# Sharing one value tile between two batches in the cross-attention of a Perceiver block

## The chip, the cores and the metric

One NeuronCore of a Trainium2 chip runs the whole block as one program. The metric is device time in microseconds, the median of several runs. The engines are TensorE (PE; its weight loads are shown apart as PEld), VectorE (DVE), ScalarE (ACT), GpSimd (POOL) and SyncE (SP, which only issues DMAs here).

## The reference, cut to what matters

```python
x = x + _L0_xattn_ref(_layernorm(x), ctx_1024, Wq, bq, Wkv, bkv, Wout, bout)   # x (16, 64, 512), ctx (16, 1601, 512)
x = x + _L0_attn_ref(_layernorm(x), ...)       # linear attention over 64 rows of each batch
x = x + _L0_ffn_ref(_layernorm(x), ...)        # 8 experts, top 2

def _L0_xattn_ref(query, context, ...):        # 16 heads of 32
    q = query @ Wq + bq
    kv = context @ Wkv + bkv                   # k and v interleaved in the last axis
    scores = jnp.einsum('bhid,bhjd->bhij', q, k) * SCALE
    attn = jax.nn.softmax(scores, axis=-1)
    out = jnp.einsum('bhij,bhjd->bhid', attn, v)
    return out @ Wout + bout
```

The change touches only the computation of `v = context @ Wv`: 16 batches of 1601 context rows each.

## The kernel before

The cross-attention takes most of the time, and it is the only part touched (`cross_attention`, L186 to L1111). All large products are made in float32r in three passes: both operands are split into a rounded part (hi) and a rest (lo), and hi*hi, hi*lo and lo*hi are added up in PSUM.

**Context.** A batch has 1601 rows, loaded transposed in four chunks of 384, 384, 384 and 450 columns into `ctx_raw`; VectorE rounds a chunk into `ctx_hi` (L577), GpSimd subtracts to get `ctx_lo` (L493).

**Units.** Keys and values of a batch are made in NU = 29 units of twelve matmuls (4 slices of the model dimension, three passes; L960). 16 are K units (a chunk times 128 dimensions, moving operand 384 or 450 columns). 13 are V units (L953 to L958): there the context tile is the stationary operand, 128 context rows, and the 512 columns of Wv move. 1601 = 12 x 128 + 65, so the 13th V unit has only 65 stationary columns (`TAIL`, `rows`). A unit writes one of two PSUM banks in turn (`ps_kv`); ScalarE copies it out to `k_t` or `v` (`copy_unit`, L818 and L822). A unit waits for the copy of the unit two before it (L944). The semaphores `kv_done` and `kv_copied` count units, 29 to a batch.

**Pairs.** The attention of a batch goes through 8 pairs of heads. For pair p of batch b TensorE does, in this order (`batch`, L1008 to L1027): transposes of the probabilities, groups 0, 1 and 2 (`turn`), the scores of the next pair (`scores`, L974), the transposes of group 3, and the product with the values (`values`, L986). In the four gaps it does units of the *next* batch: one K unit after group 0, one after group 1, a V unit after group 3, and in some pairs a second V unit after the product. Which pairs have two is in `BEHIND` (L92): the 1st, 3rd, 5th, 7th and 8th. The last chunk's units stand in the 7th and 8th pair: V units 9 and 10 in the 7th, 11 and 12 (the tail) in the 8th. ScalarE copies the V units of a pair right after the exponential of the next pair (L857 to L860).

**Beside it.** VectorE in a pair: the outputs of the pair before (L596 to L601, which free the PSUM bank `ps_o` for transpose group 1), the rests of the four probability groups (L652), the row maximum (L636), the rounding of the keys of two pairs on (`k_parts`, L588), and in the 1st, 3rd, 5th and 7th pair the rounding of a context chunk (L577). GpSimd: the rest of the values (`v_parts`, L516), the rest of the keys (L504), the rest of the context chunk (L493). SyncE issues the loads, each behind the wait that frees its buffer, strictly in the order of its queue.

**Start.** The units of batch 0 (`START`) run before any attention, with the layer norm, its transposes and the query projection between them (`start_steps`, L313). The queries go to DRAM (L471) and come back as blocks (`load_q`, L389); `FIRST_SCORES` = 26 is the unit ahead of which the first scores are made. Batch 0 then runs alone, batches 1 to 14 in a loop of 7 rounds of two, and batch 15 in `last_batch`.

## Time and profile before

| | |
|---|---|
| median of three runs | 2359.82 us (2358.14 to 2363.23) |
| the profiled execution | 2358.58 us, span 2356.8 us |
| granted TensorE clock, mean | 0.987 |
| TensorE busy | 2274.6 us, 97% |
| VectorE, ScalarE, GpSimd busy | 57%, 44%, 47% |
| start, batches, rest | to 124 us; 124 to about 1840 us; to the end |

In the rows below a time is in microseconds from the start of the span. A timeline row has the start, the duration, the engine, the line, the operation with output<-inputs and shapes, and how often it stands in a row; in brackets is the idle time of the engine before it and what ended it. A matmul's duration is modelled to its end, so in a stream of matmuls the distance of two starts tells what one costs.

### The profile page before, as it was taken

Reading aid. Unit: us, or ns where it says so; the run is one execution under the profiler, and the core shown is the slowest. Engines: PE = TensorE matmul, PEld = TensorE weight load, DVE = VectorE, ACT = ScalarE, POOL = GpSimd, SP = SyncE. Lnnn points to the kernel's source line nnn. Section 1 sums busy time; section 2 is a strip of 40 time slices with the busy share of each in tenths; the row PEclk is TensorE's granted clock in tenths of the full one; section 3 lists DMA queues with packets and bytes.
Section 4 is the critical chain, followed back from the end, with each engine's and each line's share of the span. In section 5 each row is a group of like instructions: output and inputs, shape, how many; then the busy total and the mean of one; then the engine's idle time right before and its main releaser. Section 6 shows DMA issues by size and latency. Waiting matters only on the chain. (4 is left out here: it accounts for less than half of the span.)

```text
span 2356.8 us, 37225 instructions
## 1 busy us (share of the span) xinstructions
PE 2274.6 (97%) x12921; PEld 1981.8 (84%) x12921; DVE 1348.1 (57%) x2112; ACT 1036.2 (44%) x1737; POOL 1105.3 (47%) x454
## 2 busy tenths in 40 slices
PE   8999999999999999999999999999998897799997
PEld 7688889888888889888888888888875686788886
DVE  3155655565655656565656556565667546756653
ACT  3154444444444444444444444444444421545443
POOL 2155455454455455555555555555556202533333
PEclk9999999999999999999999999999999998999999
DMA  4212111121111112111121111121131102855654
GB/s 145 96 48 57 51 48 46 49 63 50 48 47 48 45 53 66 48 46 49 47 58 52 51 48 45 53 62 52 46 114 37 39 20 103 248 172 187 193 157 92
DMA packets 141464, 175.61 MB, mean 75 GB/s; under 512 B 81600, under 2 KB 105024, under 8 KB 141248
## 3 DMA queue, kind: packets, MB, share of 16 engines
q1 hardware_dynamic: 132352, 147.37, 20.8%
q10 hardware_dynamic: 4608, 16.78, 2.2%
q0 software_dynamic: 4288, 8.67, 1.7%
q8 instruction: 125, 2.05, 0.4%
q14 instruction: 91, 0.75, 0.1%
HBM read 135.12 MB, written 37.65 MB: 73 GB/s over the span
## 5 line engine op out<-in xcount | busy, mean ns | idle before, releaser
L504 POOL TENSOR_TENSOR k_parts<-k_t,k_parts 64x1602 fp32r<-64x1602 f32 x128 | 436.9, 3413 | 717.3 <-DVE k_parts L588 717.3
L960 PE MATMUL ps_kv<-ctx_hi,wk_hi 128*128 128x384 f32 (+1 forms) x1024 | 376.0, 367 | 8.8 <-DVE ctx_lo L785 8.8
L652 DVE TENSOR_TENSOR probs_t<-ps_pt,probs_t 128x512 fp32r<-128x512 f32 x376 | 207.6, 552 | 275.4 <-ACT probs_t L830 273.9
L960 PE MATMUL ps_kv<-ctx_lo,wk_hi 128*128 128x384 f32 (+1 forms) x1024 | 352.9, 345 | 0.0
L960 PE MATMUL ps_kv<-ctx_hi,wk_lo 128*128 128x384 f32 (+1 forms) x1024 | 352.9, 345 | 0.0
L960 PE MATMUL ps_kv<-wv_hi,ctx_hi 128*128 128x512 f32 (+1 forms) x832 | 343.0, 412 | 0.6 <-DVE wv_lo L755 0.6
L960 PE MATMUL ps_kv<-wv_lo,ctx_hi 128*128 128x512 f32 (+1 forms) x832 | 330.6, 397 | 0.0
L960 PE MATMUL ps_kv<-wv_hi,ctx_lo 128*128 128x512 f32 (+1 forms) x832 | 326.4, 392 | 0.0
L838 ACT ACTIVATE probs_both<-ps_s,neg_max 128x1601 f32<-128x1601 f32 x128 | 205.0, 1602 | 178.8 <-DVE neg_max L638 178.8
L818 ACT ACTIVATE k_t<-ps_kv,bk_sb 128x384 f32<-128x384 f32 (+1 forms) x256 | 152.5, 596 | 293.3 <-PE ps_kv L960 293.2
L493 POOL TENSOR_TENSOR ctx_lo<-ctx_raw,ctx_hi 128x1536 fp32r<-128x1536 f32 (+1 forms) x64 | 233.4, 3647 | 86.0 <-DVE ctx_hi L577 84.6
L516 POOL TENSOR_TENSOR v_parts<-v,v_parts 128x832 fp32r<-128x832 f32 x120 | 237.3, 1977 | 70.4 <-ACT v_parts L848 57.2
L830 ACT CAST probs_t<-ps_pt 128x512 fp32r<-128x512 f32 x376 | 178.3, 474 | 190.5 <-PE ps_pt L1005 175.6
L636 DVE TENSOR_REDUCE row_max<-ps_s 128x1 f32<-128x1601 f32 x128 | 233.5, 1824 | 22.0 <-PE ps_s L974 9.2
L822 ACT COPY v<-ps_kv 128x512 f32<-128x512 f32 (+1 forms) x208 | 120.8, 581 | 278.3 <-PE ps_kv L960 278.3
L986 PEld LDWEIGHTS ps_o<-probs_t,v_parts 128*128 128x128 f32 (+1 forms) x1664 | 214.4, 190 | 19.8 <-DVE probs_t L652 8.9
L974 PE MATMUL ps_s<-k_parts,q_blocks 128*128 128x512 f32 (+2 forms) x1024 | 221.4, 359 | 5.1 <-DMA q_blocks<-q_parts 4.2
L986 PE MATMUL ps_o<-probs_t,v_parts 128*128 128x256 f32 (+1 forms) x1664 | 218.6, 282 | 7.5 <-DVE probs_t L652 7.5
L652 DVE TENSOR_TENSOR probs_t<-ps_o,probs_t 128x512 fp32r<-128x512 f32 x128 | 88.5, 691 | 229.7 <-ACT probs_t L830 229.5
L960 PEld LDWEIGHTS ps_kv<-ctx_hi,wk_hi 128*128 128x128 f32 x1024 | 193.6, 189 | 13.2 <-issue 9.5
L960 PEld LDWEIGHTS ps_kv<-ctx_lo,wk_hi 128*128 128x128 f32 x1024 | 194.4, 190 | 3.8 <-issue 0.7
L1005 PE MATMUL ps_pt<-ident,probs_both 128*128 128x128 f32 x1120 | 190.5, 278 | 6.0 <-DVE probs_t L652 3.8
(315 smaller groups left out, 4071.7 us busy)
## 6 DMA issues: line engine op xcount, KB each, us to landing
ctx_raw<-ctx_dram SPq DMA_DIRECT2D x49, 768.0 KB, 4.6
w_raw<-w_dram SPq DMA_DIRECT2D x64, 512.0 KB
rows_in<-zeros SPq DMA_DIRECT2D x150, 128.0 KB, 4.0
w_raw<-w_dram ACTq DMA_DIRECT2D x32, 512.0 KB
ctx_raw<-ctx_dram SPq DMA_DIRECT2D x16, 900.0 KB, 4.8
q_blocks<-q_parts SPq DMA_DIRECT2D x256, 32.0 KB, 2.3
rows<-rows_in SPq DMA_DIRECT2D x8, 768.0 KB
q_parts<-probs_t SPq DMA_DIRECT2D x16, 256.0 KB, 2.0
```

The lines of the kernel that those rows point to most:

```text
L493: nc.gpsimd.tensor_tensor(ctx_lo[c % 2][:, 0:w], ctx_raw[c % 2][:, 0:w], ctx_hi[c % 2][:, 0:w].bitcast(F32), ALU.subtract).then_inc(ctx_lo ...
L504: nc.gpsimd.tensor_tensor(k_parts[64 - 64 * s:128 - 64 * s, :], k_t[par][64 * s:64 * s + 64, g, :], k_parts[64 * s:64 * s + 64, :].bitcast ...
L516: nc.gpsimd.tensor_tensor(v_parts[:, :, 1, :], v[par][:, :, 64 * p:64 * p + 64], v_parts[:, :, 0, :].bitcast(F32), ALU.subtract).then_inc( ...
L636: nc.vector.tensor_reduce(row_max[:, q:q + 1], ps_s[:, S0:S0 + LC], AX.X, ALU.max).then_inc(max_done, 1)
L652: nc.vector.tensor_tensor(probs_t[0:m, j:j + k, 1, :], ps_turned[kv][g][0:m, 0:k, :], probs_t[0:m, j:j + k, 0, :].bitcast(F32), ALU.subtra ...
L818: nc.scalar.activation(k_t[par][:, which, CW * c:CW * c + w], ps_kv[bank][:, 0:w], ACT.Identity, bias=bk_sb[:, which:which + 1]).then_inc( ...
L830: nc.scalar.copy(probs_t[0:m, j:j + k, 0, :], ps_turned[kv][g][0:m, 0:k, :]).then_inc(pt_hi_done, 1)
L838: nc.scalar.activation(probs[q], ps_s[:, S0:S0 + LC], ACT.Exp, bias=neg_max[:, q:q + 1], scale=SCALE, accum_out=row_sum[:, q:q + 1]).then_ ...
L960: last = nc.tensor.matmul(o, still, moving, start=(k == 0 and i == 0), stop=(k == DT - 1 and i == 2))
L974: last = nc.tensor.matmul(ps_s[:, c0:c1], q_blocks[half][:, p % 4, part, :], k_parts[:, c0 - S0:c1 - S0], start=(part == 0), stop=(part == 1))
L986: last = nc.tensor.matmul(ps_o[:, 0:2], v_parts[0:m, j, :, :].rearrange("p a b -> p (a b)"), probs_t[0:m, j, :, :], start=(j == 0), stop=( ...
L1005: last = nc.tensor.transpose(ps_turned[kv][g][0:m, i, :], probs[q][:, j * P:j * P + m], ident[:])
```

## The change

Batches are taken in twos, an even one and the odd one behind it. The 65 tail rows of the even batch and the first 63 tail rows of the odd one become one tile of 128 context rows. It is made by a unit of a new kind, "T", in the place of the even batch's tail unit; SyncE later moves rows 65 to 127 of the result from the even batch's `v` to the odd one's. The last 2 rows of each odd batch, 16 in all (`ENDS`), are made in one go at the start, by twelve matmuls with 16 stationary columns (`values_of_ends`), written to DRAM and fetched two at a time. An odd batch thus has 12 V units: the unit V 10 is left out behind the product of the 7th pair, and V 10 and V 11 take the two V places of the 8th. The counters still go up by 29 for a batch: the unit ahead of the missing one counts 2.

The tiles for this, `tail_raw`/`tail_lo` and `tail_hi`, are separate from the chunks (512 + 64 columns): loaded in the 2nd pair of an odd batch, rounded by VectorE and subtracted by GpSimd in its 4th. `...` marks what is left out.

```diff
-    vs = [("V", min(j * P // CW, CHUNKS - 1), j) for j in range(JT)]
+    vs = [("V", j * P // CW, j) for j in range(JT - 1)] + [("T", CHUNKS - 1, JT - 1)]
...
+SKIPPED = UNITS.index(("V", CHUNKS - 1, JT - 3))
+UNITS_ODD = UNITS[:SKIPPED] + [None] + UNITS[SKIPPED + 1:-2] + [("V", CHUNKS - 1, JT - 3), ("V", CHUNKS - 1, JT - 2)]
...
+        TURN_FROM, QUERY_FROM, ENDS_FROM = 8, 16, FIRST_SCORES - 1
+        ends = o_t[0:ENDS].rearrange("p g c -> p (g c)")
+        ends_bank = ps_s[0:ENDS, 3 * BANK:4 * BANK]
...
+                if u == ENDS_FROM:
+                    yield "ends", 0
...
+            def units_ended(par, n):
+                return 2 if par == 1 and n == SKIPPED - 1 else 1
...
+            def load_tails(b):                       # SyncE
+                if positive(b):
+                    sp.wait_ge(kv_done, NU * (b - 1))
+                sp.dma_start(tail_raw[:], tails[b] if isinstance(b, int) else tails[bass.ds(b, 1)].rearrange("a p n -> (a p) n")
+                             ).then_inc(tail_loaded, 16)
+            def move_tails(b):
+                sp.wait_ge(kv_copied, NU * b)
+                sp.wait_ge(moved, 16)
+                if positive(b - 1):
+                    sp.wait_ge(v_lo_done, PAIRS * (b - 1))
+                half = TAIL - 2
+                sp.dma_start(v[1][0:half, JT - 1, :], v[0][TAIL:P, JT - 1, :]).then_inc(moved, 16)
+                sp.dma_start(v[1][half:TAIL, JT - 1, :], ends_v[bass.ds(b - 1, 2), :]).then_inc(moved, 16)
...
+                    if p == 2 and par == 0:
+                        move_tails(b + 1)
+                    if p == 1 and par == 1:
+                        load_tails(b + 1)
...
+            sp.wait_ge(w_hi_done, DT + 2)            # start, ahead of load_q(0, 0)
+            sp.dma_start(ends_v, ends).then_inc(moved, 16)
...
+            def split_tails(b):                      # GpSimd, after k_parts of p == 3, par == 1
+                pool.wait_ge(tail_hi_done, b + 2)
+                nc.gpsimd.tensor_tensor(tail_lo[:], tail_raw[:], tail_hi[:].bitcast(F32), ALU.subtract
+                                        ).then_inc(tail_lo_done, 2)
...
+            def round_tails(b):                      # VectorE, after rest(n, 3), before split_k, p == 3, par == 1
+                dve.wait_ge(tail_loaded, 8 * (b + 2))
+                nc.vector.tensor_copy(tail_hi[:], tail_raw[:]).then_inc(tail_hi_done, 2)
...
+                elif kind == "T":                    # ScalarE, copy_unit
+                    if positive(b):
+                        act.wait_ge(moved, 16 + 16 * b)
+                    nc.scalar.copy(v[par][:, which, :], ps_kv[bank][:]).then_inc(kv_copied, 1)
...
+                    if par == 1:                     # ScalarE, round_v at p == 0
+                        act.wait_ge(moved, 16 + 16 * (b + 1))
...
+                    if k == ENDS_FROM:               # ScalarE, start
+                        nc.scalar.copy(ends, ends_bank).then_inc(w_hi_done, 1)
...
+                if kind == "T":                      # TensorE, unit
+                    pe.wait_ge(tail_lo_done, b + 2)
...
+            def values_of_ends():
+                pe.wait_ge(tail_lo_done, 2)
+                pe.wait_ge(q_hi_done, NQ)
+                pe.wait_ge(q_lo_done, NQ)
+                for k in range(DT):
+                    hi, lo = (part[:, DT * P + k * ENDS:DT * P + (k + 1) * ENDS] for part in (tail_hi, tail_lo))
+                    for i, (still, moving) in enumerate([(hi, wv_hi), (hi, wv_lo), (lo, wv_hi)]):
+                        nc.tensor.matmul(ends_bank, still, moving[:, k, :], start=(k == 0 and i == 0),
+                                         stop=(k == DT - 1 and i == 2))
...
                 elif kind == "scores":
+                    pe.wait_ge(w_hi_done, DT + 2)
```

The words behind a `#` in the diff say only which engine or place a cut piece belongs to.

## Rows read from the trace of the kernel before

**Rows 1.** Stretches: window, length, each engine's busy time, clock, DMA

```profile
core 0: us, PE busy (x) PEld busy (x) DVE busy (x) ACT busy (x) POOL busy (x), PEclk, DMA share, GB/s
124.00:1752.00 1628.00, 1625.83 (x9298) 1434.09 (x9297) 960.24 (x1410) 748.70 (x1275) 865.95 (x300) 1.00 0.18 51
```

**Rows 2.** Stretches: a pair with one V unit, one with two

```profile
1057.79:1069.39 11.60, 11.60 (x72) 10.59 (x70) 6.41 (x11) 6.39 (x11) 7.13 (x3) 1.00 0.06 6
1043.36:1057.79 14.43, 14.43 (x84) 12.80 (x83) 9.63 (x13) 5.91 (x10) 7.56 (x3) 1.00 0.30 96
```

**Rows 3.** Timeline of TensorE, end of a seventh pair and after

```profile
1081.78 0.40 PE L960 MATMUL ps_kv<-wv_hi,ctx_hi 128*128 128x512 f32 x1
...
1084.59 0.60 PE L1005 MATMUL ps_pt<-ident,probs_both 128*128 128x128 f32 x4
1084.94 0.45 PE L960 MATMUL ps_kv<-ctx_hi,wk_hi 128*128 128x450 f32 x1
...
1087.48 0.60 PE L1005 MATMUL ps_o<-ident,probs_both 128*128 128x128 f32 x4
```

**Rows 4.** Timeline of TensorE, the last K matmul, first scores

```profile
106.26 0.37 PE L960 MATMUL ps_kv<-ctx_hi,wk_lo 128*128 128x450 f32 x1
110.87 3.01 PE L974 MATMUL ps_s<-k_parts,q_blocks 128*128 128x290 f32 x8 [4.24 <-DMA q_blocks<-q_parts]
```

**Rows 5.** Stretches, from the first scores on

```profile
110.87:116.66 5.79, 5.79 (x16) 4.74 (x16) 2.68 (x3) 0.00 (x0) 0.84 (x1) 0.50 0.24 62
```

**Rows 6.** Timeline of ScalarE, copy of the seventh pair's first V unit

```profile
1080.93 0.57 ACT L822 COPY v<-ps_kv 128x512 f32<-128x512 f32 x1
```

**Rows 7.** Timeline of VectorE, seventh and eighth pair

```profile
1082.17 0.94 DVE L577 CAST ctx_hi<-ctx_raw 128x1536 fp32r<-128x1536 f32 x1
...
1083.92 0.28 DVE L601 TENSOR_TENSOR o_t<-ps_o,o_mid 64x128 f32<-64x128 f32 x1
...
1091.71 0.69 DVE L652 TENSOR_TENSOR probs_t<-ps_pt,probs_t 128x512 fp32r<-128x512 f32 x1 [2.20 <-ACT probs_t L830]
```

**Rows 8.** Timeline of TensorE's weight loads, eighth pair

```profile
1092.46 0.14 PEld L1005 LDWEIGHTS ps_pt<-ident,probs_both 128*65 128x65 f32 x1 [0.36 <-DVE probs_t L652]
1095.19 1.71 PEld L986 LDWEIGHTS ps_o<-probs_t,v_parts 128*128 128x128 f32 x13
```

**Rows 9.** Timeline of GpSimd, seventh and eighth pair

```profile
1082.32 4.31 POOL L504 TENSOR_TENSOR k_parts<-k_t,k_parts 64x1602 fp32r<-64x1602 f32 x1 [8.88 <-DVE k_parts L588]
1086.71 3.52 POOL L493 TENSOR_TENSOR ctx_lo<-ctx_raw,ctx_hi 128x1536 fp32r<-128x1536 f32 x1
1090.31 1.97 POOL L516 TENSOR_TENSOR v_parts<-v,v_parts 128x832 fp32r<-128x832 f32 x1
```

**Rows 10.** Groups by shape: count, busy us, mean ns, V units

```profile
L960 PE MATMUL ps_kv<-wv_hi,ctx_lo 128*128 128x512 f32 x768 | 301.3, 392 | 0.0
...
L960 PE MATMUL ps_kv<-wv_hi,ctx_lo 128*65 128x512 f32 x64 | 25.1, 393 | 0.0
...
L960 PEld LDWEIGHTS ps_kv<-wv_hi,ctx_lo 128*128 128x128 f32 x768 | 144.7, 188 | 34.1
...
L960 PEld LDWEIGHTS ps_kv<-wv_hi,ctx_lo 128*65 128x65 f32 x64 | 8.7, 136 | 6.2
```

**Rows 11.** Timelines of VectorE and GpSimd, fifth pair, GpSimd first

```profile
1054.39 3.35 DVE L577 CAST ctx_hi<-ctx_raw 128x1800 fp32r<-128x1800 f32 x1
...
1053.77 3.02 POOL L504 TENSOR_TENSOR k_parts<-k_t,k_parts 64x1602 fp32r<-64x1602 f32 x1 [5.73 <-DVE k_parts L588]
```

**Rows 12.** Timelines of ScalarE and SyncE's queue at the start

```profile
106.67 0.64 ACT L818 ACTIVATE k_t<-ps_kv,bk_sb 128x450 f32<-128x450 f32 x1 [1.87 <-PE ps_kv L960]
...
105.75 7.47 SPq L389 DMA_DIRECT2D q_blocks<-q_parts  x16
```

**Rows 13.** Timelines of VectorE and GpSimd at the start

```profile
59.94 0.75 DVE L778 SCALAR_TENSOR_TENSOR probs_t<-ps_s,bq_sb,probs_t 128x512 fp32r<-128x512 f32 x1 [6.08 <-ACT probs_t L929]
...
103.88 4.26 POOL L504 TENSOR_TENSOR k_parts<-k_t,k_parts 64x1602 fp32r<-64x1602 f32 x1 [45.92 <-DVE k_parts L588]
```

More of the change, by code:

```diff
@@ L116 @@
 LAST = CHUNKS - 1
-START += [unit for g in range(DT) for unit in (("K", LAST, g), ("V", LAST, JT - DT + g))]
+START += [unit for g in range(DT) for unit in (("K", LAST, g), ("V" if g < DT - 1 else "T", LAST, JT - DT + g))]
 START_LAST_OF_CHUNK = [max(n for n, u in enumerate(START) if u[1] == c) for c in range(CHUNKS)]
@@ L346, in later, with unit_of, has_unit @@
             return None if isinstance(b, int) and b == B - 1 else (b + 1, 1 - par, p + steps - PAIRS)
+        def unit_of(b, par, n):
+            if isinstance(b, int) and b == 0:
+                return START[n]
+            return UNITS_ODD[n] if par == 1 else UNITS[n]
+        def has_unit(par, n):
+            return par == 0 or n != SKIPPED
+        def units_ended(par, n):
+            return 2 if par == 1 and n == SKIPPED - 1 else 1
         def splits_at(b, p, kv):
@@ L522, in batch @@
                         chunks = chunks + 1
+                    if p == TAILS_AT and par == 1:
+                        pool.wait_ge(k_lo_done, n + 3)
+                        pool.wait_ge(ctx_lo_done, chunks)
+                        split_tails(b + 1)
             def last_batch(b, par):
@@ L671, in batch @@
                     rest(n, 3, kv)
+                    if p == TAILS_AT and par == 1:
+                        round_tails(b + 1)
                     if two_on and p != PAIRS - 2:
@@ L807, in copy_unit @@
             def copy_unit(b, par, n):
-                kind, c, which = START[n] if isinstance(b, int) and b == 0 else UNITS[n]
+                kind, c, which = unit_of(b, par, n)
                 bank = (NU * par + n) % 2
@@ L819, in copy_unit @@
                                          bias=bk_sb[:, which:which + 1]).then_inc(kv_copied, 1)
+                elif kind == "T":
+                    if positive(b):
+                        act.wait_ge(moved, 16 + 16 * b)
+                    nc.scalar.copy(v[par][:, which, :], ps_kv[bank][:]).then_inc(kv_copied, 1)
                 else:
                     m = rows(which)
-                    nc.scalar.copy(v[par][0:m, which, :], ps_kv[bank][0:m, :]).then_inc(kv_copied, 1)
+                    nc.scalar.copy(v[par][0:m, which, :], ps_kv[bank][0:m, :]).then_inc(kv_copied, units_ended(par, n))
             def copy_group(n, g, kv):
@@ L915, in _ @@
                         nc.scalar.activation(std[:], std[:], ACT.Sqrt).then_inc(std_done, 1)
+                    if k == ENDS_FROM:
+                        nc.scalar.copy(ends, ends_bank).then_inc(w_hi_done, 1)
                 elif kind == "exponent":
                     exponent(0, 0)
-                elif kind == "scores":
+                elif kind in ("scores", "ends"):
                     pass
@@ L935, in unit @@
             def unit(b, par, n):
-                order = START if isinstance(b, int) and b == 0 else UNITS
-                kind, c, which = order[n]
+                kind, c, which = unit_of(b, par, n)
+                former = unit_of(b, par, n - 2 if n - 1 == SKIPPED and par == 1 else n - 1) if n else None
                 bank = ps_kv[(NU * par + n) % 2]
-                if n == 0 or order[n - 1][1] != c:
+                if kind == "T":
+                    pe.wait_ge(tail_lo_done, b + 2)
+                elif n == 0 or former[1] != c:
                     pe.wait_ge(ctx_lo_done, CHUNKS * b + c + 1)
@@ L952, in unit @@
                         passes = [(wk_hi[:, k, dims], hi), (wk_hi[:, k, dims], lo), (wk_lo[:, k, dims], hi)]
+                    elif kind == "T":
+                        o, tile = bank[:], slice(k * P, (k + 1) * P)
+                        passes = [(tail_hi[:, tile], wv_hi[:, k, :]), (tail_hi[:, tile], wv_lo[:, k, :]),
+                                  (tail_lo[:, tile], wv_hi[:, k, :])]
                     else:
@@ L1014, in beside @@
                         for u in AT[p][gap] if kv else ():
-                            unit(b + 1, 1 - par, u)
+                            if has_unit(1 - par, u):
+                                unit(b + 1, 1 - par, u)
                     turn(n, p % 2, 0, kv)
@@ L1085, in _ @@
                     unit(0, 0, k)
+                elif kind == "ends":
+                    values_of_ends()
                 elif kind == "scores":
+                    pe.wait_ge(w_hi_done, DT + 2)
                     pe.wait_ge(q_lo_done, NQ)
@@ L2259 @@
                           for c in range(CHUNKS)], axis=2)
+    by_dim = np.asarray(ctx_1024).transpose(0, 2, 1).reshape(B, DT, P, LC)
+    tails = np.zeros((B, P, TAIL_W), np.float32)
+    even = by_dim[0::2, :, :, LC - TAIL:]
+    odd = by_dim[1::2, :, :, LC - TAIL:]
+    tails[0::2, :, :DT * P] = np.concatenate([even, odd[:, :, :, :TAIL - 2]], axis=3).transpose(0, 2, 1, 3).reshape(B // 2, P, -1)
+    tails[0, :, DT * P:] = odd[:, :, :, TAIL - 2:].transpose(2, 1, 0, 3).reshape(P, -1)
     wkv = np.asarray(L0_xattn_Wkv).reshape(D, D, 2)
```

34 lines of the change are left out of this document (25 added, 9 removed).

## The prediction, written before the result was known

> **What bounds the kernel now.** I read the stretch view of the attention stage first: from 124 to 1752 us TensorE is busy 1625.83 of 1628.00 us at a granted clock of 1.00 (the 2.4 GHz level), while VectorE, ScalarE and GpSimd are busy 960, 749 and 866 us [rows 1]. So the stage is paced by TensorE's instruction stream, and work taken out of that stream is worth its full issue time, as long as nothing else turns out to be late. The second view is the same one for two neighbouring pairs of one batch: a pair with one value unit behind its last transpose takes 11.60 us, a pair with two takes 14.43 us, and TensorE is busy for all of both [rows 2]. The difference, 2.83 us, is the price of a value unit at the place where the change takes one out. The timeline of TensorE gives the same from inside: the second value unit of a seventh pair starts at 1081.78 and the next transpose at 1084.59, 2.81 us for twelve matmuls [rows 3]. I use 2.82. The start, before 124 us, is bounded otherwise: there TensorE sits idle 4.24 us for the first query blocks and then runs at the 1.2 GHz level [rows 4, 5].
>
> **Removed.** Odd batches 1, 3, ... 15 compute 12 value units where they had 13; their units are computed during the batch before, so the hole is in the seventh pair (p = 6) of batches 0, 2, ... 14: eight holes. 8 x 2.82 = 22.6 us off TensorE. The ScalarE copy of each unit goes too (0.57 us each, the length of the copy in [rows 6]); ScalarE is not the bound and that is worth nothing.
>
> **What is late next, at the hole.** I redo the eighth pair with TensorE 2.81 us earlier, from the rows of one even batch (the loop repeats the same code for the others). (a) The first transpose would start at 1081.78, the old start of the removed unit. It needs the exponential, done before 1080.93, when ScalarE goes on to its next copy [rows 6]. (b) The K unit behind it starts 0.35 later, at 1082.13. It now takes the bank of the unit just before it and so waits for that unit's copy: 1080.93 + 0.57 = 1081.50 [rows 6]. 0.6 us to spare. (c) The second transpose group would start at 1087.48 - 2.81 = 1084.67 [rows 3] and needs the outputs of the pair before; VectorE ends them at 1083.92 + 0.28 = 1084.20 [rows 7]. VectorE takes them up right behind its context cast and not because of TensorE, so they come no earlier than now: 0.4 us to spare. (d) The product with the values would begin loading weights at 1095.19 - 2.81 = 1092.38 [rows 8]. It needs GpSimd's low half of the values. GpSimd runs three operations without a gap, 1082.32 to 1092.28 [rows 9], started by VectorE's cast and independent of the hole, so this end does not move. From a VectorE end at 1091.71 + 0.69 = 1092.40 to the weight load it releases at 1092.46 is 0.06 us [rows 7, 8]; 1092.28 + 0.06 = 1092.34 against 1092.38. This is the tightest place, a tie: cost 0.0, bound 0.3 us per hole because GpSimd's spans are rough, so 0 to 2.4 us in all. I take 0, since the two rows leave 0.04. (e) The eighth pair's own k_parts cast on VectorE moves up to about 1091.9 and finds GpSimd busy until 1092.28; it waits 0.4 us, which lies before a whole pair of cover.
>
> **Replaced.** In even batches the 65-row unit becomes a 128-row one of the same twelve matmuls with 512 moving columns. The weight load grows from 136 to 188 ns, but the matmuls last 393 ns with 65 columns of weights and 392 with 128 [rows 10]: cost 0. (The Trainium skill speaks against that. TensorE: Matmul & The Clock Gate, Part 3, The mechanism, says that a weight load overlaps matmuls in flight only when it goes to another row group, and the section on LDWEIGHTS that its time goes with the columns. That is a rival below; these rows speak against it here.)
>
> **Added in the loop, once in two batches.** VectorE rounds 576 columns: between 0.94 x 576/1536 = 0.35 us [rows 7] and, if GpSimd holds it up, 3.35 us [rows 11]. It comes in the fourth pair, one with a single value unit; such a pair has VectorE busy 6.41 and GpSimd 7.13 of 11.60 us [rows 2]. I take 0.35, as the cast comes before GpSimd is handed anything. Queued behind it on VectorE is the k_parts cast, and behind that GpSimd's half and the scores of the next pair, which have the slack of a whole pair. GpSimd subtracts 576 columns: 3.52 x 576/1536 = 1.3 us [rows 9], at most 4.3, behind k_parts and ahead of v_parts; 7.13 + 1.3 is still under 11.60. Cost 0; if that cover were gone it would be 7 x 1.3 = 9 us. SyncE gets one load of 288 KB and two moves; their waits are for units and copies finished a batch ago, and the rows are read most of a batch later. ScalarE's and TensorE's new waits are for the same things. Cost 0.
>
> **Added at the start.** Twelve matmuls for the 16 left-over rows: 2.81 us, between a value and a K unit. But more hangs on them. Now the last K unit's last matmul starts at 106.26 and its copy at 106.67 (0.64 long); SyncE issues the query loads at 105.75, and the scores start 5.12 us later, at 110.87 [rows 4, 12]. After: the K unit's copy starts at 106.67 + 2.81 = 109.48, the copy of the left-over rows follows it, 0.64 and 0.57 us [rows 6] to 110.69. SyncE's new wait stands ahead of the query loads: 0.06 us to be released, as above, and 0.47 to issue the store (a query load takes 7.47/16 = 0.47), so the first query load goes out near 111.2 instead of 105.75. The scores move by the same 5.5 us, to 116.4; of this 2.8 is matmuls and 2.7 longer idling. TensorE's clock is 0.50 for 5.79 us after today's 4.24 us of idling [rows 5]; I expect the same after 7 us. Its loss now is half of 5.79, 2.9 us; by where the clock comes back it could be 1.5 less or more. The tail's round and subtract before the queries fit into 6.08 us in which VectorE and 45.92 us in which GpSimd wait [rows 13]. So the start costs 5.5, with ends 4.0 and 7.0.
>
> **Sum.** -22.6 + 5.5 = -17.1 us. The profiled run took 2358.58 us (span 2356.8 and 1.8 around it) and would take 2341.5. It lay 1.2 under the median of the three runs, 2359.82; the forecast is for a median: 2359.8 - 17.1 = **2342.7 us**. Everything behind 1752 us is started by ends of this stage and moves with it.
>
> **Rivals.**
> 1. The tie at (d), and (c), go the wrong way: the hole is partly filled by a wait of TensorE for GpSimd's v_parts. 0.3 to 0.9 us in each of eight pairs, 2345 to 2350 us. For it: 0.04 us of room; against: GpSimd's spans do not depend on the hole, and the removed time may come out at 2.81 and not more.
> 2. The change ends slower: the context cast in the seventh pair loses its race with GpSimd's k_parts. Today VectorE starts it at 1082.17 and GpSimd starts at 1082.32, the cast takes 0.94 [rows 7, 9]; where GpSimd is first, it takes 3.35 [rows 11]. (The Trainium skill, SBUF — State Buffer, Who interferes with whom, calls this an exclusive lock held for a whole instruction by whichever engine issues first; these rows agree.) If it lost, it would end at 1086.3 to 1086.8 (GpSimd's k_parts from 1082.32, 3.02 long as in [rows 11] or 3.52, the 4.31 of today less the 0.79 shared with the cast, and then 0.94), the outputs 1.1 later at 1087.4 to 1087.9, and the second transpose would wait 2.7 to 3.2 us: all of the hole. Against the 2.82 taken out that is between -0.1 and +0.4 per hole, up to 3 us in all; with the start 2359.8 + 5.5 + 2 = 2367. It decides as soon as GpSimd starts ahead of the cast. Against: the removed unit comes after this race and shifts neither side.
> 3. Wider weights show: (188 - 136) ns x 12 x 8 = 5.0 us, so 2347.7.
> 4. The start is dearer, the clock staying down longer or the store delaying the loads: 2344.7 to 2347.
> 5. The change does not do what it says, since the moves hold up ScalarE at the head of an odd batch and the hole is paid there: 2365. Against: over 60 us lie between move and use.
>
> **Chances.** Forecast (2340.5 to 2344.7) 0.72; rival 1 0.12; rival 3 0.02; rival 4 0.07; rival 2 0.05; rival 5 0.02. A measurement of this kernel can tell about 0.2%, 4.7 us, from no change. Faster: 0.72 + 0.12 + 0.02 + 0.07 = 0.93, of which I put 0.02 to no change for the upper ends of 1 and 4 together. The same 0.02, slower 0.07. The range for 8 in 10: down to 2339 (start at its low end, and the runs before spread by 5 us), up to 2350 (rival 1's end).
>
> **What would show it.** Right: in even batches the eighth pair begins 2.8 us sooner after the seventh than in odd ones, with TensorE idle under 0.3 us before its transposes and products; the stretch of the attention stage from its first transpose is 22.6 us shorter; the first scores start near 116.4 us, with the new matmuls at 104.0; value matmuls still start every 0.23 us. Wrong: a wait of TensorE for v_parts or o_t that occurs eight times; a context cast of over 3 us in the seventh pair of even batches; GpSimd's v_parts late in the fifth pair of odd batches; a start that moves by over 7 us.

## The result, and the profile after

| | before | after |
|---|---|---|
| median, us | 2358.98 (2357.17 to 2363.23, 4 runs) | 2338.86 (2336.51 to 2340.62, 4 runs) |
| profiled execution, span | 2358.58, 2356.8 | 2336.51, 2334.8 |
| granted TensorE clock, mean | 0.987 | 0.987 |
| TensorE matmuls | 12921 | 12837 |

The ratio is 0.9908, with a 95% interval of 0.9896 to 0.992: 20.1 us faster. The forecast was 2342.7 us, 3.8 us too high. The time lies 1.6 us under the range of 2340.5 to 2344.7, and 0.14 us under the wider one for 8 in 10, which began at 2339.

The stretch view shows where the 22.0 us between the two spans are. The columns are those of [rows 1]; the first row is the attention stage, from ScalarE's first rounding of the values (batch 0) to that of batch 15, the second is everything behind it.

```profile
127.46:1733.12 1605.66, 1602.50 (x9202) 1424.62 (x9202) 962.59 (x1417) 745.55 (x1268) 875.72 (x307) 1.00 0.19 53
...
1733.12:2334.80 601.68, 537.59 (x3166) 462.58 (x3165) 357.82 (x653) 250.93 (x405) 212.74 (x137) 0.96 0.43 131
```

The same two stretches of the kernel before, cut at the same instructions:

```profile
124.30:1752.25 1627.95, 1625.78 (x9298) 1433.99 (x9297) 960.48 (x1411) 748.62 (x1275) 865.95 (x300) 1.00 0.18 51
...
1752.25:2356.80 604.55, 538.21 (x3166) 462.69 (x3164) 356.06 (x652) 250.93 (x405) 213.20 (x137) 0.95 0.43 130
```

The stage begins 3.16 us later, is 22.29 us shorter, and what follows it is 2.87 us shorter: 3.16 - 22.29 - 2.87 = -22.0. The last number is a surprise, as the change touches nothing there: the same 3166 matmuls, 0.6 us less busy, and the rest is idle time.

**At the hole.** The timelines after, of the pair that answers to [rows 3, 7, 9], TensorE first, then its weight loads, VectorE and GpSimd:

```profile
1072.06 1.70 PE L1091 MATMUL ps_o<-probs_t,v_parts 128*128 128x256 f32 x13
1073.60 0.60 PE L1110 MATMUL ps_pt<-ident,probs_both 128*128 128x128 f32 x4
...
1076.49 0.60 PE L1110 MATMUL ps_o<-ident,probs_both 128*128 128x128 f32 x4
...
1084.22 1.72 PEld L1091 LDWEIGHTS ps_o<-probs_t,v_parts 128*128 128x128 f32 x13
...
1073.97 0.95 DVE L646 CAST ctx_hi<-ctx_raw 128x1536 fp32r<-128x1536 f32 x1
...
1075.72 0.28 DVE L675 TENSOR_TENSOR o_t<-ps_o,o_mid 64x128 f32<-64x128 f32 x1
...
1074.13 4.31 POOL L560 TENSOR_TENSOR k_parts<-k_t,k_parts 64x1602 fp32r<-64x1602 f32 x1 [8.86 <-DVE k_parts L657]
...
1082.09 1.98 POOL L579 TENSOR_TENSOR v_parts<-v,v_parts 128x832 fp32r<-128x832 f32 x1
```

The transposes stand right behind the product (13 matmuls, 1.54 us), with no idle time in brackets anywhere. The outputs end at 1076.00, the transposes that need them start at 1076.49; GpSimd ends the values' low half at 1084.07, the weights that need it load at 1084.22. The seventh pair takes 12.37 to 12.40 us where it took 15.21 to 15.24, in all eight even batches.

**At the start.** TensorE, ScalarE and SyncE's queue:

```profile
103.05 0.39 PE L1066 MATMUL ps_s<-wv_hi,tail_hi 128*16 128x512 f32 x1
...
108.10 0.37 PE L1054 MATMUL ps_kv<-ctx_hi,wk_lo 128*128 128x450 f32 x1
115.44 2.99 PE L1079 MATMUL ps_s<-k_parts,q_blocks 128*128 128x290 f32 x8 [6.98 <-DMA q_blocks<-q_parts]
118.25 0.42 PE L1054 MATMUL ps_kv<-wv_hi,ctx_hi 128*128 128x512 f32 x1
...
109.04 0.56 ACT L1003 COPY o_t<-ps_s 16x512 f32<-16x512 f32 x1
...
109.62 0.34 SPq L529 DMA_DIRECT2D ends_v<-o_t  x1
110.16 7.46 SPq L438 DMA_DIRECT2D q_blocks<-q_parts  x16
```

The queries leave SyncE behind the store of the ends, and the scores wait 6.98 us for them instead of 4.24 [rows 4].

### The profile page after: what moved, and what is told of

Read it like the earlier page. It is cut to its first block and busy times, and to the rows that moved or that the text cites. A ratio compares the mean times of both kernels' runs of the same rounds, so it can differ in the third digit from the quotient of the medians.

```text
span 2334.8 us, 37197 instructions
## 1 busy us (share of the span) xinstructions
PE 2251.1 (96%) x12837; PEld 1972.3 (84%) x12837; DVE 1355.8 (58%) x2120; ACT 1033.6 (44%) x1730; POOL 1116.1 (48%) x462
## 5 line engine op out<-in xcount | busy, mean ns | idle before, releaser
L1054 PE MATMUL ps_kv<-wv_hi,ctx_hi 128*128 128x512 f32 x768 | 316.6, 412 | 0.6 <-DVE wv_lo L833 0.6
L1054 PE MATMUL ps_kv<-wv_lo,ctx_hi 128*128 128x512 f32 x768 | 304.2, 396 | 0.0
L1054 PE MATMUL ps_kv<-wv_hi,ctx_lo 128*128 128x512 f32 x768 | 301.0, 392 | 0.0
L905 ACT COPY v<-ps_kv 128x512 f32<-128x512 f32 x192 | 111.7, 582 | 228.2 <-PE ps_kv L1054 228.2
```

The lines of the kernel that those rows point to most:

```text
L1054: last = nc.tensor.matmul(o, still, moving, start=(k == 0 and i == 0), stop=(k == DT - 1 and i == 2))
```

## The experiments

The first four ran on one chip with 2359.41 us for the kernel before, the next four with 2359.45, then three with 2360.02 and two with 2360.31.

### The changed kernel again

> The changed kernel once more, unaltered. The forecast's sum was -17.1 us against the kernel before, the first measurement -20.1. Theory A (the sum left something out at the start, 1 to 2 us, because TensorE's clock comes back sooner after the scores): about -18.5 again, and the profile again shows the clock at half for about 3 us from the first scores on, where the kernel before had 5.8. Theory B (that, and a gain of 2 to 3 us behind the attention stage that belongs to the change): -20 to -22 and the stretch from the last batch to the end again near 601.7 us (before: 604.6). If that stretch is back near 604, the difference there was the spread between executions.

2337.07 us (2336.51 to 2337.72), ratio 0.9905 (0.989 to 0.992). The stage took 1605.59 us and the rest 601.3, so both shortenings belong to the program and not to one execution. This run is the base of those below.

### Ends stored behind the query loads

```diff
-            sp.wait_ge(w_hi_done, DT + 2)
-            sp.dma_start(ends_v, ends).then_inc(moved, 16)
...
             load_q(0, 0)
             load_q(0, 1)
+            sp.wait_ge(w_hi_done, DT + 2)
+            sp.dma_start(ends_v, ends).then_inc(moved, 16)
```

> SyncE's wait for the left-over rows and their store stand behind the query loads of the start instead of ahead of them; nothing else is changed. If the start's 5.5 us come from the place in SyncE's queue as in the forecast, the query loads go out when the queries are stored, the scores wait only for ScalarE's copy of the left-over rows, about 1.4 us behind the last K unit, and start 5.5 us sooner; the clock then has no reason to fall, worth another 1.4 to 2.9 us. 7 to 8 us faster than the changed kernel. If the start costs because of the twelve matmuls and not because of the queue, it is within 3 us of it.

2331.74 us (2329.8 to 2334.1), ratio 0.9883 (0.9868 to 0.9899), 5.3 us under the changed kernel, where 7 to 8 was expected, and the fastest version of the study. TensorE's first scores and SyncE's queue:

```profile
110.31 1.73 PE L1079 MATMUL ps_s<-k_parts,q_blocks 128*128 128x290 f32 x8 [1.71 <-DMA q_blocks<-q_parts]
...
104.94 7.46 SPq L438 DMA_DIRECT2D q_blocks<-q_parts  x16
112.44 0.43 SPq L535 DMA_DIRECT2D ends_v<-o_t  x1
```

The wait falls from 7.0 to 1.7 us, and the eight score matmuls take 1.73 us instead of 3: the clock stays at its 2.4 GHz level. The stage begins at 121.08, 8.0 us sooner than in the run before (129.07), as expected; 2.1 us of it are lost again behind (stage 0.9 longer, rest 1.2).

### The hole filled again

```diff
-UNITS_ODD = UNITS[:SKIPPED] + [None] + UNITS[SKIPPED + 1:-2] + [("V", CHUNKS - 1, JT - 3), ("V", CHUNKS - 1, JT - 2)]
+UNITS_ODD = UNITS[:SKIPPED + 1] + UNITS[SKIPPED + 1:-2] + [("V", CHUNKS - 1, JT - 3), ("V", CHUNKS - 1, JT - 2)]
```

(with `has_unit` always true and `units_ended` always 1.)

> The changed kernel with the hole filled: odd batches compute value unit 10 in the seventh pair as well and once more in the eighth, so 13 value units; the result is the same. Everything else of the change stays. By the forecast each hole is worth 2.82 us and nothing fills it: 8 x 2.82 = 22.6 us slower than the changed kernel, which leaves it 2 to 5 us slower than the kernel before (the start). If waits had filled part of the hole, less than 22.6; if the change gained elsewhere in the loop, it ends faster than the kernel before.

2374.98 us (2373.07 to 2377.04), ratio 1.007 (1.0056 to 1.0084): 37.9 us over the changed kernel, where 22.6 was expected. The seventh pairs are back at 15.21 us, so the price of the holes is right. The other 12.7 us in the spans are in two places where nothing was edited: the rest takes 605.3 us instead of 601.3, and the loop's six back edges lose more. In the two pairs around a back edge (the last of an even batch and the first of the next odd one) TensorE's work takes 29.56 us; this is what such two pairs take inside the loop's body. Here they take 31.63 on average, in the changed kernel 30.17 and in the kernel before 29.99. One of them in each, before, after and filled:

```profile
868.72:898.58 29.86, 29.71 (x167) 25.22 (x166) 17.28 (x25) 12.91 (x23) 16.29 (x7) 1.00 0.17 52
```

```profile
860.26:890.42 30.16, 29.79 (x167) 25.87 (x166) 18.55 (x29) 12.91 (x24) 19.10 (x7) 1.00 0.21 61
```

```profile
875.95:907.30 31.35, 29.86 (x167) 25.83 (x166) 17.29 (x25) 13.01 (x23) 16.25 (x7) 1.00 0.21 59
```

All have the same 167 matmuls; the third has 1.5 us in which TensorE does nothing. The timeline puts 1.40 us of that to "issue", a wait for nothing that the profile shows. This is what the later runs are about.

### Keys ahead of the outputs in the seventh pair

```diff
-                    if two_on and p != PAIRS - 2:
+                    if two_on:
                         split_k(*two_on)
...
-                    if two_on and p == PAIRS - 2:
-                        split_k(*two_on)
```

> The changed kernel with VectorE's rounding of the keys in the seventh pair ahead of the reciprocal, as in all other pairs, so that GpSimd starts its k_parts about 1.7 us sooner, ahead of VectorE's context cast. The forecast's rival 2: the cast then waits for GpSimd and ends at 1084.6 to 1085.1 in the times of the rows, the outputs end 1.1 later, and the second transpose group, due at 1084.67, is late by 1.0 to 1.5 us in each of the eight seventh pairs with a hole: 8 to 12 us slower than the changed kernel, and the cast in the profile over 3 us. If the two engines do not exclude each other there, no difference.

2353.95 us (2350.68 to 2356.4), ratio 0.9974 (0.9963 to 0.9986), 16.9 over the changed kernel, where 8 to 12 was expected. TensorE, VectorE and GpSimd at the eighth pair of an even batch:

```profile
1089.22 0.66 PE L1108 MATMUL ps_o<-ident,probs_both 128*128 128x128 f32 x4 [1.30 <-DVE o_t L675]
...
1084.25 3.82 DVE L646 CAST ctx_hi<-ctx_raw 128x1536 fp32r<-128x1536 f32 x1
1088.88 0.28 DVE L675 TENSOR_TENSOR o_t<-ps_o,o_mid 64x128 f32<-64x128 f32 x1
...
1083.60 3.66 POOL L560 TENSOR_TENSOR k_parts<-k_t,k_parts 64x1602 fp32r<-64x1602 f32 x1 [7.08 <-DVE k_parts L657]
```

This is the race of rival 2, lost on purpose. GpSimd starts first, the context cast takes 3.82 us instead of 0.95, the outputs end late and TensorE waits 1.30 us, in each of the eight batches. It costs 1.5 us a time, 12 in all; the other 5 us are again at the back edges (32.48 us, 1.5 of which is this wait). The edit is in VectorE's part alone, so TensorE's instructions are those of the changed kernel, as many and in the same order; yet two of the six back edges have a second stop on "issue" (0.81 and 1.43 us) that the changed kernel doesn't have.

### The same order in the kernel before

> The kernel before with VectorE's order of the seventh pair made like that of the others (rounding of the next keys ahead of the reciprocal and the output's eviction). In the changed kernel the same edit cost 17 us in all, with TensorE idle 1.3 us at the second group of transposes in each of 8 seventh pairs. Theory: in the kernel before the unit in the seventh pair covers it, 0 to 2 us (2359 to 2361 us). Rival, the order costs by itself, whatever covers it: 2370 us or more, with the same idle time.

2359.42 us (2357.56 to 2363.96), ratio 1.0 (0.9991 to 1.0009). The race is lost here too, and costs nothing: the cast takes 3.80 us, the outputs end at 1086.46, and TensorE, with the V unit still ahead of it, doesn't ask for them before 1087.85. The unit was the cover, and the change spends it.

```profile
1081.57 3.80 DVE L577 CAST ctx_hi<-ctx_raw 128x1536 fp32r<-128x1536 f32 x1
1086.18 0.28 DVE L601 TENSOR_TENSOR o_t<-ps_o,o_mid 64x128 f32<-64x128 f32 x1
...
1087.85 0.60 PE L1003 MATMUL ps_o<-ident,probs_both 128*128 128x128 f32 x4
```

### The hole in the eighth pair

```diff
-SKIPPED = UNITS.index(("V", CHUNKS - 1, JT - 3))
-UNITS_ODD = UNITS[:SKIPPED] + [None] + UNITS[SKIPPED + 1:-2] + [("V", CHUNKS - 1, JT - 3), ("V", CHUNKS - 1, JT - 2)]
+SKIPPED = UNITS.index(("T", CHUNKS - 1, JT - 1))
+UNITS_ODD = UNITS[:SKIPPED] + [None]
```

> As the changed kernel, but the unit left out is the one in the eighth pair (the tail unit of odd batches, in the gap behind the value product), and V10 stays in the seventh pair. The tail of the odd batch isn't computed at all here (its value rows come from the even batch), as in the changed kernel. Prediction's theory (a hole shows its full 2.82 us only where nothing else is late behind it): the seventh pair goes back to 15.2 us; the eighth, which is also the loop's back edge for half of the batches, becomes 12.4 us only if what it covered (VectorE's value split and the scores' evictions for the next batch) fits: I expect 5 to 17 us more than the changed kernel, 2344 to 2356 us. Rival, any place is as good: 2337 us within 2.

2358.23 us (2356.12 to 2361.14), ratio 0.9994 (0.9985 to 1.0003): as slow as the kernel before, 21.2 over the changed one, more than I expected. Batch 0, which no back edge follows, has its eighth pair at 12.33 us where the changed kernel has 15.19, and gives 1.1 us of that back in the pair behind it. At the six back edges the two pairs take 30.17 us, what they take in the changed kernel, with twelve matmuls fewer:

```profile
871.34:901.51 30.17, 27.16 (x155) 23.64 (x154) 17.09 (x25) 12.53 (x22) 16.15 (x7) 1.00 0.21 61
```

Another of them shows both parts of the time in which TensorE is idle, and behind them VectorE's step that the second part goes back to:

```profile
1101.55 0.65 PE L1110 MATMUL ps_pt<-ident,probs_both 128*128 128x128 f32 x4 [1.62 <-issue]
...
1105.04 0.66 PE L1110 MATMUL ps_o<-ident,probs_both 128*128 128x128 f32 x4 [0.74 <-DVE o_t L675]
...
1103.92 0.43 DVE L670 TENSOR_REDUCE o_low<-ps_o 64x128 f32<-64x256 f32 x1 [4.62 <-issue]
```

VectorE has a stop of its own at the back edge. Between the two batches of one round of the loop it takes up the outputs 0.04 us after the end of the value product. At a back edge it takes them up 2.2 to 2.6 us after it, in the kernel before and in the changed kernel alike, with "issue" as the only reason. There the value unit behind the product covers this stop. With the unit gone the outputs come 4.0 to 5.0 us after the product, and TensorE waits 0.74 to 1.73 us for them in all six, besides its own stop of 1.55 to 1.93. So 6 x 2.8 = 17 us are lost at the back edges. The rest is 3.4 us longer (604.7 us), because the last hole, in batch 14, is worth only 0.3 us: where the unit stood TensorE waits 2.33 us for GpSimd's keys, which the next scores need. Work taken out beside this back edge is worth nothing here.

### Where TensorE's code lies

Five kernels have waits added that are met already, ahead of TensorE's first unit, and nothing else:

```diff
             pe.wait_ge(ident_made, 2)
+            for _ in range(27):
+                pe.wait_ge(ident_made, 2)
```

The trace shows one instruction for each two of them: 14 for 27, 115 for 229, 14 for 28, 32 for 64.

> The kernel before, with 27 waits ahead of TensorE's first unit that are met already (the semaphore of the identity matrix, which TensorE has just waited for). TensorE idles there for its first weights, so the waits cost nothing themselves; what they do is move all later TensorE code by the 27 instructions that the change also puts ahead of the loop (12 matmuls with their weight loads and 3 waits). Theory code position: the unexplained part of the run with the filled hole (some 12 us at the loop's back edge and 3 us behind the attention stage, over its 22.6 us of holes) comes from where TensorE's loop lies in its instruction blocks. Then this kernel, with before's work, loses 1 to 2 us at each of the 6 back edges: 2365 to 2375 us, and the two pairs around the back edge go from 29.99 us to 31 or more. Rival, the added work on VectorE and GpSimd (tails) costs it: this kernel stays at 2359 us within its spread of 2 us, and the two pairs at 30.0 us.

> The run with the filled hole again (odd batches compute V10 twice, so the saving of the loop is gone), with 229 met waits ahead of TensorE's first unit: with the 27 instructions that the change adds there they make 256, a whole 16 KB block of instructions at 64 bytes each, if the waits are of that size, so that the loop lies in its blocks as in the kernel before. Theory code position: the loss at the back edges goes back to that of before (two pairs around it 29.99 us instead of 31.63), and the time from 2375 us to 2362 to 2366 us (before + start 3 to 5). Rival, VectorE's and GpSimd's added work: 2375 us again, 31.6 us at the back edge.

> The changed kernel with 64 met waits ahead of TensorE's first unit, nothing else: they stand in the trace as half as many instructions (27 waits were 14 more, 229 were 115 more), so TensorE's later code moves by 32 instructions. Theory code position: the stretch behind the attention stage, 601.3 and 601.7 us in two executions of the changed kernel, and the two pairs at the back edge, 30.17 us, both change by more than they differ between executions of the same code (0.4 and 0.01 us), with nothing else changed; by how much and which way I can't say ahead: 2334 to 2350 us in all. Rival, those stretches follow from the change's timing and not from where code lies: 601.5 and 30.17 us again and 2337 us.

> The version with SyncE's wait and store of the ends behind the query loads (2331.7 us), with 28 met waits (14 instructions) ahead of TensorE's first unit. In the kernel before the same 14 cost 0.65 us at each back edge and 3.2 us behind the attention stage, by the traces, and 2.4 us in the medians. Theory code position: another loop, another place, so the sign is open; the stretch behind the attention stage changes from 602.6 us by 1 us or more: 2328 to 2340 us. Rival: 2331.7 us within 1.

> The same version with 64 met waits (32 instructions): 2328 to 2345 us by the theory of code position, and its stretch behind the attention stage and its back edges equal to those of the changed kernel with 64 waits (within 1 us and 0.2 us), since TensorE's code is the same in both; the difference between those two is then the 5.3 us of the late ends again (2337.07 against 2331.74 us).

| kernel | instructions | median, us | the two pairs at a back edge, mean (range) | rest |
|---|---|---|---|---|
| before | 0 | 2359.4 | 29.99 (29.86 to 30.20) | 604.6 |
| before | +14 | 2361.81 (2359.25 to 2366.04) | 30.65 (30.03 to 30.97) | 607.8 |
| hole filled | 0 | 2374.98 | 31.63 (30.95 to 32.06) | 605.3 |
| hole filled | +115 | 2365.20 (2362.69 to 2366.70, and one of 2825.39) | 29.98 (29.80 to 30.18) | 601.6 |
| after | 0 | 2337.07 | 30.17 (29.89 to 30.61) | 601.7, 601.3 |
| after | +32 | 2368.68 (2364.93 to 2370.42) | 34.88 (34.04 to 36.86) | 605.5 |
| ends late | 0 | 2331.74 | 30.37 (29.96 to 30.59) | 602.5 |
| ends late | +14 | 2345.48 (2337.62 to 2348.3) | 32.06 (30.30 to 34.82) | 608.3 |
| ends late | +32 | 2368.26 (2356.88 to 2371.76) | 35.95 (34.03 to 37.56) | 608.7 |

The pairs and the rest are from the profiled execution of each, cut at ScalarE's first rounding of the values in a pair. It was the slowest of its kernel in the rows of after +32 and ends late +14 and +32, 2.5 us over the median in before +14, and the fastest of its kernel in hole filled. The executions of ends late +32 lie 15 us apart, with one and the same code.

The change's whole gain is undone by 32 instructions that do nothing.

Going through the expectations: the filled hole does come back by 10 us, with 5.4 us of the waits themselves still in it (its first unit starts at 14.07 instead of 8.69 us, as 115 instructions have to be gone through), though by 115 instructions and not by a whole block; the arithmetic of the block was wrong. The 14 in the kernel before cost 2.4 us in the medians and nothing that can be told from its spread (ratio 1.0004, 0.9995 to 1.0013), with both places longer in the trace, far from the 10 I had named. With 32 the changed kernel loses 31.6 us, which was above my range. The two kernels with 32 were expected to be alike in both places, and 5.3 us apart: they differ by 3.2 us in the rest and by 1.1 at a back edge, and their medians by 0.4. So the loss isn't set by the position alone, which the 15 us between executions of one code say too, and so does the run with the keys first.

What a back edge looks like in the changed kernel with 32 instructions, TensorE, then three stretches of it:

```profile
886.14 0.65 PE L1110 MATMUL ps_pt<-ident,probs_both 128*128 128x128 f32 x4 [0.78 <-issue]
886.55 0.42 PE L1054 MATMUL ps_kv<-ctx_hi,wk_hi 128*128 128x384 f32 x1
886.81 0.34 PE L1054 MATMUL ps_kv<-ctx_lo,wk_hi 128*128 128x384 f32 x1
889.11 0.48 PE L1054 MATMUL ps_kv<-ctx_hi,wk_lo 128*128 128x384 f32 x1 [1.97 <-issue]
```

```profile
871.16:905.20 34.04, 31.25 (x167) 27.21 (x166) 18.54 (x29) 13.01 (x24) 19.06 (x7) 0.95 0.20 54
886.14:889.11 2.97, 1.00 (x6) 0.86 (x7) 1.66 (x3) 0.94 (x2) 0.00 (x0) 0.92 0.83 268
889.11:892.19 3.08, 3.08 (x11) 3.04 (x10) 0.37 (x1) 0.43 (x1) 1.96 (x1) 0.52 0.66 149
```

TensorE stops in the middle of a unit, between two matmuls that need nothing new: 0.78 us before the batch's first transposes, 1.97 after the second matmul of its first K unit. Then the clock is at 0.52, the 1.2 GHz level, for 3.08 us, which costs 1.5 more. Together 4.3 of the 4.5 us that this back edge is over 29.56. In the changed kernel the same place has 0.34 us before the transposes and nothing after.

What TensorE stands for can be read from the packets of the queue of kind "instruction", q8, each of 16 KB. In the stop above one runs from 886.71 to 887.77, and TensorE goes on 1.34 us after its end. So it is with all 21 second stops of 1.7 us and more at the back edges of the kernels with 14 or 32 instructions added, the run below included: each ends 1.1 to 1.7 us after the end of such a packet. In the four longest, of 3.6 to 3.9 us, the packet starts 1.4 to 1.6 us after TensorE has stopped, in the others 0.2 us after at the latest.

(The Trainium skill, Runtime: NRT & Kernel Launch, Instruction fetch mechanics, says that each engine's instructions come by DMA in blocks of 16 KiB, one ahead, that crossing into a block is mostly hidden, and that a taken branch out of the blocks at hand has to wait for its target. These traces agree: the packets have that size, and the stops are at the loop's branch and end behind a packet. For the length of a stop the page has no number.)

### Is it the context load?

At that moment SyncE issues the next context load, 768 KB, at 885.55, and the DMA engines are busy for 0.83 of the stretch in which TensorE stands. It could be that the instructions queue behind it. One K unit more in SyncE's wait puts the load behind the stop:

```diff
-                    sp.wait_ge(kv_done, NU * freed + lasts[at] + 1)
+                    sp.wait_ge(kv_done, NU * freed + lasts[at] + (2 if at == CHUNKS - 1 else 1))
```

> The changed kernel with 64 met waits (2368.68 us), and in addition SyncE issues the context load of each batch's first pair one K unit later. In the run with 64 met waits TensorE stands 0.8 and 2.0 us without a releaser around the loop's back edge; the load of 768 KB goes out at 885.55, between the two, and while TensorE stands the second time the DMA engines are 83% busy with it, as one 16 KB block of instructions (1.06 us) is fetched. Afterwards the clock is at its 1.2 GHz level for 3.1 us. Theory contention: the instruction block waits behind the load's packets; with the load behind it the second gap shrinks from 2.0-3.9 us to under 1 and the clock doesn't fall: 6 x 3 to 4 us less, 2345 to 2352 us. Rival, latency alone: the gap follows from where the code lies, TensorE reaching a block that isn't there, and no load has a part in it: 2368 us within 2, same gaps. The context itself isn't needed until VectorE rounds it at the end of the pair, some 5 us after it lands.

2366.85 us (2362.83 to 2370.69), ratio 1.0025 (1.0016 to 1.0035): 1.8 less, not 17 to 24. The chips differ too, by 0.3 us for the kernel before, and the two intervals overlap, so the 1.8 us aren't clear of noise. The stretch that answers to the second of the three above, and the matmul at its end:

```profile
885.51:888.48 2.97, 1.01 (x6) 0.86 (x7) 1.83 (x3) 1.06 (x2) 0.00 (x0) 0.90 0.03 8
...
888.48 0.48 PE L1054 MATMUL ps_kv<-ctx_hi,wk_lo 128*128 128x384 f32 x1 [1.96 <-issue]
```

With the DMA engines at 0.03 instead of 0.83 the stop is 1.96 us instead of 1.97. But 1.97 is the shortest of the six in the run before: there they are 2.35, 2.51, 1.97, 3.89, 2.10 and 2.51 us, and here 1.96, 1.97, 1.96, 1.70, 1.69 and 1.96. The packet of instructions now starts 0.5 to 0.6 us before TensorE stops, in all six; with the load beside it it started between 0.6 us before and 1.6 after. So contention is not the cause of the stop, some 1.7 to 2.0 us of which stay without it; by these two executions it adds 0.7 us on average and 1.9 in the longest. The stops before the transposes are 0.2 us longer in exchange, and the two pairs take 34.28 us on average instead of 34.88, 3.6 us in all six.

> The fastest version so far (ends stored behind the query loads, 2331.74 us) with the same later context load and no extra waits. Its back edges lose only about 0.6 us each. Theory contention: up to 6 x 0.5 us less, 2328.5 to 2331; rival latency alone: 2331.7 within 1.

2332.61 us (2329.6 to 2334.37), ratio 0.9878 (0.9864 to 0.9892), against 2331.74: no difference that can be measured. In its profiled execution the clock did fall at the first scores, to 0.50 from 111.77 to 115.18, after 1.83 us of idling; in those of the three other kernels with the ends stored late it stayed up after 1.4 to 1.7. So the clock's part of the gain of the ends stored late isn't there in every execution.

## Why the prediction was right or wrong

**The bound and the price of the holes: right.** 15.22 - 12.40 = 2.82 us in each of eight seventh pairs, 22.6 us. The stage is 22.3 us shorter: another 0.8 comes in pieces of some hundredths of a microsecond, most of them in the pairs with two value units, for which I have no cause, and 6 x 0.18 = 1.1 goes at the back edges.

**What is late next: right, by small margins.** (c) had 0.4 us foreseen and has 0.49. (d), the tie, had 0.04 and has 0.15. Rival 1 is out. Rival 2 didn't occur, but its mechanism is real: forced, it cost 1.5 us per hole in the changed kernel and nothing in the kernel before. I had priced its wait at 2.7 to 3.2 us, and it was 1.30. The chain from GpSimd's start to the end of the outputs was as long as I had put it, 5.6 us (1083.60 to 1089.16). But the order of that run lets GpSimd start 4.32 us before TensorE is due at the second transposes (1089.22 - 1.30), and I had reckoned with 2.35 (1082.32 to 1084.67).

**Wider weights: right, cost 0.** The T units' matmuls take 396 ns where those of the V units take 392, and start every 0.23 us; with 16 stationary columns they start every 0.23 us too (the 12 of the start, 103.05 to 105.83). Rival 3 is out.

```profile
L1054 PE MATMUL ps_kv<-wv_hi,tail_lo 128*128 128x512 f32 x32 | 12.7, 396 | 0.0
```

**Added in the loop: right.** No wait of TensorE on the tails, the moves or GpSimd in the stage. GpSimd is 9.8 us busier there.

**The start: mechanism right, one term too large.** The matmuls cost 2.78 us and the idle time grows by 6.98 - 4.24 = 2.74, in all 5.5 as forecast; ends stored late gave it back. (The whole start ran 0.95 us earlier in this execution: 108.10 - 2.78 against 106.26 [rows 4].) The term that failed is "I expect the same after 7 us", that the clock comes back 5.79 us after the scores' start [rows 5]. It came back after 2.81 (the step from 115.44 to 118.25), which saves half of 2.98, 1.5 us. I had counted the low stretch from the scores' start, and it doesn't begin there. It begins in the idle time before them. Before and after, with the columns of [rows 1]:

```profile
109.93:116.76 6.83, 5.89 (x16) 4.87 (x17) 2.78 (x3) 0.00 (x0) 1.78 (x1) 0.50 0.25 63
```

```profile
111.46:118.29 6.83, 2.85 (x9) 2.50 (x10) 0.00 (x0) 0.00 (x0) 0.00 (x0) 0.50 0.30 68
```

The granted clock is at 0.50, the 1.2 GHz level, for 6.83 us in both. In the kernel before TensorE works through 5.89 of them and in the changed one, whose idle time is longer, through 2.85. In the nine other profiled executions with such a pause the low stretch is 6.83 us long in eight and 10.24 in one, and begins after 2.0 to 4.3 us of idling. So what is left of it behind the scores' start differs from one execution to the next: 5.8, 5.3 and 4.5 us in three with the start of the kernel before, 2.8 and 4.0 in the changed kernel. I had taken the value of one execution for a rule.

**The sum: one step failed.** "Everything behind 1752 us is started by ends of this stage and moves with it" is true of the data and not of the time. The rest is 2.9 us shorter, with the same work: in the kernel before TensorE stands near its end, where the program branches around its second loop, for

```profile
2306.13 0.38 PE L2035 MATMUL ps_pair<-w_hi,rows_hi 128*128 128x256 f32 x1 [1.35 <-issue]
2308.86 0.50 PE L2056 MATMUL ps_one<-w_hi,y_hi 128*128 128x512 f32 x1 [1.04 <-issue]
```

and after only once, for 0.81 us. That is 1.6 of the 2.9 us. Another 1.0 is two waits for VectorE, 1.70 and 0.56 us before and 1.17 and 0.10 after; both are shorter still in the run of the kernel before with the keys first, so they differ between executions of one TensorE code. The stops do go with the code's position. The one of 1.04 us stands in both executions with the TensorE code of the kernel before and in no other, and waits that are met already make stops there and nothing else is changed: +14 instructions make the rest of the kernel before 607.8 us, with a stop of 2.04, and +32 make that of the changed kernel 605.5. The position isn't all of it: with the TensorE code of the changed kernel the rest was 601.7, 601.3 and 601.3 us, but 602.5 and 602.3 with the ends stored late. What makes these 1.0 us is open.

The forecast for this execution was 2341.5 and it took 2336.5. Of the 5.0, 2.9 is the rest, 1.5 the clock and 0.95 the earlier start, less 0.3 for the stage.

**What the range left out.** The change adds 27 TensorE instructions at the start (twelve matmuls, their weight loads and three waits), takes 24 out of batch 0, which stands ahead of the loop, and 24 out of the loop's body, so the loop begins 3 instructions later, and its end and all code behind it lie 21 earlier. No rival had a price for that. In this execution 1.1 us were lost at the back edges and 2.9 gained behind; at other positions of the changed kernel and of its version with the ends late the runs above show 32 and 14 us more.

## What to carry to other kernels

Taking a unit of work out of the engine that paces a stage is worth its full issue time only where each neighbour's next deadline has been redone with it gone: the same unit was worth 2.82 us in the seventh pair and nothing beside the back edge, and the order of two VectorE steps that had cost nothing under its cover cost 12 us without it. A new store goes behind the loads that somebody waits for: 5.3 us here. And before a few microseconds are put to an edit in a long program with a loop, move the code by some instructions that do nothing and time that too; a change that adds or removes instructions ahead of a loop moves the loop too, and here that alone cost up to 36.5 us.

## What the runs showed of the hardware

- TensorE stops at the loop's back edge on "issue": 0 to 0.8 us in the changed kernel, and 0.4 to 1.5 and then 1.7 to 3.9 us, in the middle of a unit, with 32 instructions more. The second stop ends 1.1 to 1.7 us after the end of a 16 KB packet of the instruction queue. Without the context load beside it, it was 1.7 to 2.0 us.
- VectorE stops there as well: in the kernels before and after it takes up a finished product after 2.2 to 2.6 us at a back edge, and after 0.04 us between the two batches of one round.
- Behind a stop of 1.97 us the clock was at its 1.2 GHz level for 3.08 us, and it fell at a stop of 1.69 us too (with the late context); stops of 1.93 and 2.24 us in the run with ends late and +14 left it at 1.00. The length of the stop alone doesn't tell.
- After a pause of 4.2 to 7.2 us the clock's low stretch was 6.83 us long in ten of eleven executions, and 10.24 in one; how much of it fell on work was 2.9 to 5.9 us in the two kernels.
- VectorE's cast of 1536 columns took 0.95 us when it started 0.16 us ahead of GpSimd's k_parts (1073.97 and 1074.13) and 3.82 us when it started 0.65 behind it.

What is still open: which rule gives a position its price, since kernels with the same TensorE code differ, by 1.1 us at a back edge and 3.2 us behind with 32 instructions added; what the positions of the other engines' code cost, VectorE's above all, as no run moved them alone; and why executions of one code lie up to 15 us apart.
